# A fused layer on one core: the gather moved behind the attention scores, and coefficients made by token halves

## The reference

```
x = x + tanh(g_xattn) * attention(layernorm(x), ctx)        # 16 heads of 16
h  = silu(layernorm(x) @ W_up.T + b_up) @ W_down.T + b_down # 4096 x 128
q  = h @ W_q.T                                              # 2 x 8 heads x 64
sx, ix = top_k(q0 . keys0, 8);  sy, iy = top_k(q1 . keys1, 8)
sc, pk = top_k(sx[:, None] + sy[None, :], 8)                # 8 of 64 sums, per head
e  = (ix * 45 + iy)[pk]                                     # the chosen experts
z  = silu((h . down_embed[e]) * softmax(sc))
x  = x + tanh(g_ffn) * sum(z * up_embed[e])
```

## Time and profile before

| | |
|---|---|
| median of three runs | 1220.84 us |
| the profiled execution | 1225.47 us, span of its trace 1223.7 us |
| PE busy | 1143.9 us, 93% |
| DVE busy | 1036.6 us, 85% |
| ACT busy | 765.2 us, 63% |
| POOL busy | 332.4 us, 27% |
| longest wait of PE in a full turn | 0.7 to 0.9 us, for ACT's hT |

### The profile page before, as it was taken

How to read it: one execution, slowest core, us unless ns; L and a number is a source line. 1 busy time by engine, 2 the same in 40 slices (tenths; PEclk the granted TensorE clock), 3 DMA queues, 4 the chain that set the end, 5 groups by cost and what they waited for, 6 DMA issues and landing times. The chain is left out here.

```text
span 1223.7 us, 47668 instructions
## 1 busy us (share of the span) xinstructions
PE 1143.9 (93%) x19004; PEld 1026.9 (84%) x19004; DVE 1036.6 (85%) x4238; ACT 765.2 (63%) x2602; POOL 332.4 (27%) x149
## 2 busy tenths in 40 slices
PE   6876999999999999999999999999999999999968
PEld 4765888888889888888988888888888898888857
DVE  3477889988888898888999888879889889988992
ACT  5656666667766666766666677656676766667411
POOL 4130333321233332123333122333212333320220
PEclk9987999999999999999999999999999999999988
DMA  8034655644554564456465445645445645643581
GB/s 221 11 100 117 151 104 130 151 119 121 134 151 99 134 150 117 112 144 125 108 151 138 120 116 149 145 88 151 124 114 135 151 110 124 150 123 104 142 188 28
DMA packets 304948, 154.53 MB, mean 126 GB/s; under 512 B 282735, under 2 KB 295895, under 8 KB 296535
## 3 DMA queue, kind: packets, MB, share of 16 engines
q1 hardware_dynamic: 304727, 151.47, 50.9%
HBM read 79.62 MB, written 4.72 MB: 69 GB/s over the span
## 5 line engine op out<-in xcount | busy, mean ns | idle before, releaser
L368 POOL TENSOR_TENSOR rstd<-veps,minus_half 128x1 f32<-128x1 f32 x32 | 67.9, 2123 | 713.6 <-DVE veps L851 713.6
L1203 PE MATMUL bank<-ue,coef 128*128 128x256 f32 x1024 | 233.9, 382 | 1.4 <-ACT coef L427 1.4
L1203 PEld LDWEIGHTS bank<-ue,coef 128*128 128x128 f32 x1024 | 191.6, 192 | 25.6 <-ACT coef L427 1.6
L948 PEld LDWEIGHTS bank<-z,hot_rT 128*128 128x128 bf16 x1984 | 150.4, 96 | 22.3 <-issue 22.3
L969 PEld LDWEIGHTS bank<-uc,hot_r 128*128 128x128 bf16 x5952 | 152.4, 96 | 15.2 <-issue 15.1
L969 PE MATMUL bank<-uc,hot_r 128*128 128x32 bf16 x5952 | 155.8, 176 | 9.3 <-issue 8.4
L1015 PEld LDWEIGHTS bank<-hT,deT 128*128 128x128 f32 x1024 | 128.3, 194 | 38.7 <-ACT hT L577 29.8
L948 PE MATMUL bank<-z,hot_rT 128*128 128x32 bf16 x1984 | 156.5, 177 | 1.0 <-DVE picked L643 1.0
L948 PE MATMUL bank<-zl,hot_rT 128*128 128x32 bf16 x1984 | 155.7, 177 | 0.8 <-issue 0.8
L948 PE MATMUL bank<-zll,hot_rT 128*128 128x32 bf16 x1984 | 155.7, 177 | 0.0
L1015 PE MATMUL bank<-hT,deT 128*128 128x128 f32 x1024 | 134.3, 280 | 22.7 <-ACT hT L577 22.7
(11 more groups left out here) (161 smaller groups left out, 2269.4 us busy)
## 6 DMA issues: line engine op xcount, KB each, us to landing
hot_rT<-expert_rows SPq DMA_DIRECT2D x62, 1024.0 KB, 6.3
xt<-in_x SPq DMA_DIRECT2D x32, 128.0 KB, 2.4
out<-x1k SPq DMA_DIRECT2D x32, 128.0 KB, 2.2
ct<-in_ctx SPq DMA_DIRECT2D x32, 64.0 KB, 2.2
ue<-in_L_ffn_up_embed SPq DMA_DIRECT2D x1, 2048.0 KB, 13.4
z<-in_L_ffn_W_up SPq DMA_DIRECT2D x1, 1024.0 KB, 7.9
expert_rows<-r_h SPq DMA_DIRECT2D x64, 8.0 KB, 1.8
WupT<-expert_rows SPq DMA_DIRECT2D x1, 1024.0 KB, 4.8
```

What stands on the lines that cost most here:

```text
L368: nc.gpsimd.tensor_tensor(rstd[:, :], veps[:, :], minus_half[:, :], ALU.pow).then_inc(S["rstd_ok"], 1)
L948: last = mm(bank[:, 32 * (q - 16 * k):32 * (q - 16 * k) + 32], (last_rT_parts if T.last else hot_rT_parts)[k // 2][:, q % (Q // 2), :], pa ...
L1203: last = mm(bG0[:, 0:DM], coef[:, c, :, :].rearrange("r h q -> r (h q)"), ue[:, c, :], start=(c == 0), stop=(c == C - 1))
```

## The change

Five edits in one:

1. PE: `gather(0)` no longer stands before `scores`; all four quarters follow it.
2. DVE: both `scores_max` stand ahead of `gathered(0)`, instead of behind the first and the second pick.
3. ACT: `hT` stands ahead of `zt`, and `expert_exp` behind both.
4. DVE: `coef_parts` works on half of the slots at a time: first the three parts of half 0, then those of half 1, twelve instructions of half the size instead of six. There is a signal for each half (`uc0`, `uc1`) instead of each part.
5. PE: `scatter(0)` waits for `uc0`, `scatter(2)` for `uc1`, where `scatter(0)` waited for all three.

```
@@ ACT
-                if B and not B.last:
-                    expert_exp(B)
-                if Ct:
-                    Ct.wait("zp_ok")
-                    nc.scalar.activation(zt[:, :], zp[:, :], ACT.Tanh, scale=0.5).then_inc(S["zt_ok"], 1)
                 if Fw:
                     Fw.wait("hid_pe")
                     Fw.free("z_pe3")
                     nc.scalar.activation(hT[:, :], bD[:, 0:TILE], ACT.Identity, bias=bdn_sb[:, 0:1],
                                          scale=1.0 if Ct else 0.5).then_inc(S["hid_sb"], 1)
+                if Ct:
+                    Ct.wait("zp_ok")
+                    nc.scalar.activation(zt[:, :], zp[:, :], ACT.Tanh, scale=0.5).then_inc(S["zt_ok"], 1)
+                if B and not B.last:
+                    expert_exp(B)
@@ DVE
-                def coef_parts(n):
+                def coef_parts(qh, n):
                     Ct.wait(f"uh{n + 1}")
-                    Ct.free("w_pe3")
+                    Ct.free("w_pe1" if qh == 0 else "w_pe3")
+                    qs = slice(qh * Q // 2, (qh + 1) * Q // 2)
                     for half in range(2):
                         rows = slice(64 * half, 64 * half + 64)
-                        last = nc.vector.tensor_tensor(uc[rows, n, :, C * half:C * half + C].rearrange("s q (c b) -> s q c b", b=2),
-                                                       hot_c[rows, :, :].rearrange("s q (c b) -> s q c b", b=2),
-                                                       u_h[rows, n, :, :].unsqueeze(2).to_broadcast([64, Q, C // 2, 2]), ALU.mult)
-                    last.then_inc(S[f"uc{n}"], 1)
+                        last = nc.vector.tensor_tensor(uc[rows, n, qs, C * half:C * half + C].rearrange("s q (c b) -> s q c b", b=2),
+                                                       hot_c[rows, qs, :].rearrange("s q (c b) -> s q c b", b=2),
+                                                       u_h[rows, n, qs, :].unsqueeze(2).to_broadcast([64, Q // 2, C // 2, 2]), ALU.mult)
+                    if n == 2:
+                        last.then_inc(S[f"uc{qh}"], 1)
...
+                if A and (Ct or not Fw):
+                    scores_max(0)
+                    scores_max(1)
                 if Ct:
                     gathered(0)
-                if A and (Ct or not Fw):
-                    scores_max(0)
-                if Ct:
                     gathered(1)
-                if A and (Ct or not Fw):
-                    scores_max(1)
-                if Ct:
                     gathered_sum(0)
...
-                    coef_parts(0)
-                    coef_parts(1)
-                    coef_parts(2)
+                    for qh in range(2):
+                        for n in range(3):
+                            coef_parts(qh, n)
@@ PE
-                    if k == 0:
-                        for n in range(3):
-                            Ct.wait(f"uc{n}")
+                    if k % 2 == 0:
+                        Ct.wait(f"uc{k // 2}")
...
-                if Ct and not Ct.last:
-                    gather(Ct, cs, 0)
                 if A:
                     scores()
...
-                    for k in range(1, 4):
+                    for k in range(4):
                         gather(Ct, cs, k)
```

More of the change, by code:

```diff
@@ L195, in flamingo_layer @@
             "rows_in0 rows_in1 hotrT0 hotrT1 hotr_in0 hotr_in1 hotc g_pe0 g_pe1 g_pe2 g_pe3 gm0 gm1 gm2 gm3 zs0 zs1 zs2 zs3 zp_ok zt_ok u_ok uh1 uh2 uh3 ul_ok "
-            "uc0 uc1 uc2 w_pe0 w_pe1 w_pe2 w_pe3 w_sb0 w_sb1 w_sb2 w_sb3 out_pe y_ok y_out0 y_out1"
+            "uc0 uc1 w_pe0 w_pe1 w_pe2 w_pe3 w_sb0 w_sb1 w_sb2 w_sb3 out_pe y_ok y_out0 y_out1"
         ).split()}
@@ L763, in turn @@
                     if Ct.last:
-                        Ct.free("uc2")
+                        Ct.free("uc1")
                     nc.vector.tensor_tensor(
```

## The result

The changed kernel takes 1273.73 us (1271.29 to 1274.82, four runs) against 1220.06 us before on the same chip: ratio 1.0438, 95% interval 1.0417 to 1.0458, 53.7 us more. The forecast was 1284 us in a range of 1256 to 1309 us.

The account below looks back on a forecast made before the run. The loop from DVE's searches through ACT's silu, PE's scores and DVE's picks, u and uc was taken as the bound. 29 x (0.77 + 1.1 + 0.5), less 7.4, plus 1.6 gave +63 us: 1284 us, range 1256 to 1309 us.

Parts of the forecast that it names:

- The loop: DVE's searches, ACT's top_rep to silu, PE's scores, DVE's picks, u, uc and searches set the turn, 35.63 us.
- the second loop of the kernel before: PE's own row, nearly the same length; its one gap, 0.74 us before dense, waits for hT behind zt and zp.
- Gather and hT: Gather behind the scores makes hid late, and hT then holds back zt and DVE's u: +0.77 us a turn.
- Halves: Twelve uc instructions on DVE of 0.445 us instead of six of 0.703 us: +1.1 us a turn, in the loop.
- The halves bring nothing: An earlier scatter on PE gains nothing: PE is busy with dense(2) and nobody waited for uc.
- The clock: PE's slack before the scores drops its clock in most turns, slowing scores and gather: +0.5 us a turn, bounds 0 and 1.5.
- rival 4: The clock falls on PE's scores every turn, 1.5 us instead of 0.5: 1313 us; chance 13%.
- The turns in which PE was late: Longer turns costing 7.4 us in the kernel before, which 2.6 us of new PE slack swallow.
- The drain: One more DVE turn at the end with both costs, then PE's half clock and scatter bound: +1.6 us.

Follow-up runs that it names:

- the early table: The changed kernel with one added one-column silu in ACT's idle time, so the table load no longer stands between top_rep and up_silu(0): 1224.6 us.

## Why the prediction was right

**The loop.** Right, and it decided the sign: `smax` stood still at 8.26 us, DVE took the cost of everything behind it, and the early table moved the turn by what it took out of the chain. The longer of PE's two waits was not for `up_act`, as I had said, but most likely for `k_diag`. And the second loop of the kernel before was misread: it does not run through PE's wait for `hT`, but through `uc` and the scatter (35.52 us against 35.63). This did not touch the sum, because both costs lie in the longer loop.

**Gather and hT: +0.77 us forecast, 0.59 us measured.** The mechanism was right (`hT` holds `zt`, since `hid` is late), the term too large. Four quarters and the change to the next work take 4.83 us (629.67 to 634.50 in the turn shown), where three took 3.75 us. So the quarter that moved costs 1.08 us there, and not the 1.25 us that I had taken from a stretch with one change-over in it. `hT` starts 0.04 us after `hid`, as forecast.

**Halves: +1.1 us forecast, 0.98 us measured.** One half costs 0.433 us, the forecast had 0.445. 2 x 0.433 - 0.703 gives 0.163 us, some 157 cycles at 0.96 GHz, as the fixed part. Of the two figures in the Trainium skill, page VectorE: DVE Perf Modes, section on the TRN2 errata, the trace agrees with the 150 cycles, not with the 58 of its table.

**The halves bring nothing.** Right for the time of the changed kernel: its scatter begins 21.06 us after `top_rep` and 21.63 us with whole coefficients, but PE only waits longer in front of the masks for it. The reason given, that nobody waited for `uc`, was wrong, in the kernel before by 0.2 us and by 0.97 us as soon as PE gets faster. That this cost the forecast nothing was luck: the loop through the scatter was the shorter one by 0.11 us.

**The clock: +0.5 us a turn forecast, about 0.3 us measured.** 29 turns in 1088.73 us are 9.9 us over 29 x 37.20, 1.4 of them in the first. The mechanism was right: +1.3 us where the half clock meets the scores, 0.2 us where it meets the gather. It met the scores in a fifth of the turns, where I had assumed a quarter, and the gather in another fifth, where I had charged 0.2 us to all; I had expected a clock below 1.00 in most turns, and it was 14 of 29. That it can be nearly every turn, rival 4, was shown by the run with `hT` and halves on the kernel before.

**The turns in which PE was late.** Right: swallowed, 7.4 us. **The drain:** +1.2 us against 1.6.

Together 29 x 1.57 = 45.5, plus 9.9, less 1.2 for the cold first turn and 7.4, plus 1.2 for the drain and 0.4 for the start is 48.4 us; the spans differ by 48.5 us. The forecast's 63 us was too large by the sum of these terms (5 + 3.5 + 6 us), all of them sized at or above their row. The ones that decide the sign were read, not estimated, from offsets of 0.07 us in the trace. That the median moved by 53.7 us and the span by 48.5 us lies in the profiled execution of before, which was 4.6 us above its median.

## What to carry to other kernels

Several loops of nearly equal length can hold a software pipeline: here the loop from the searches through silu and scores (35.63 us) and the one from `uc` through the scatter (35.52 us) lay 0.1 us apart, and PE's row through `hT` reached the scatter only 0.2 us ahead of `uc`. An edit that shortens one gains nothing alone and may cost, and an edit that costs 35 us in one state is worth 15 in another; so write down the margin at each meeting point, change what stands in the longest loop first, and try small edits together. Before work is moved from in front of a wait to behind it, ask what fills the wait then.

## What was not expected of the hardware

A table load of 1.28 us between the searches and the silu was worth 49 us in the changed kernel, 41 of them by the shorter chain, and a one-column silu in idle time moves it there. In the kernel before the same silu gained 2 us. The half clock is cheap for narrow bfloat16 matmuls, 0.2 us a turn on the gather, and dear for float ones, 2.34 us against 1.12 us for the scores. With waits of PE of mostly 1.2 and 0.58 us in front of the scores the clock fell in 24 of the 28 full turns behind the first of one kernel, with mostly 1.9 and 0.58 us in 13 of 28 of the changed kernel, and with 0.2 to 0.5 and 0.58 us in none of 28 in three others. Filling the gap of the changed kernel with unneeded work ended the falls and gained 7 us.
